# Zeros for all slot lists asked for with the first loads, and the expert weights' last row taken off on TensorE behind the first routing

## The reference, cut to what matters

```
x = in_features                                    # 8 batches x 512 rows x 128
x = x + 0.5 * moe(layernorm(x))                    # "mixture 1"
x = x + attention(layernorm(x))                    # 16 heads of 8, causal, rotary
x = x + 0.5 * moe(layernorm(x))                    # "mixture 2", same weights
x = x + 0.5 * mx_linear(layernorm(x))              # weight and input on an fp6 grid
x = x + gated_scan_block(x)                        # sigmoid/tanh scan, then a SiLU block
x = x + 0.5 * mx_linear(layernorm(x))

def moe(z):                                        # 8 experts, the best 2 for each row
    s, i = top_k(z @ router_w + router_b, 2); g = softmax(s)
    return sum over k of g[k] * (relu(z @ W1[i[k]] + b1[i[k]]) @ W2[i[k]] + b2[i[k]])
```

## Time and profile before

| | us |
|---|---|
| three runs, median (lowest to highest) | 975.32 (974.37 to 977.39) |
| the profiled execution | 978.61 |
| its span | 976.8 |
| PE busy | 837.3 (86%) |
| POOL busy | 666.3 (68%) |
| DVE busy | 623.6 (64%) |
| ACT busy | 550.1 (56%) |
| granted clock of PE, mean | 0.949 of 2.4 GHz |

### The profile page before, as it was taken

The page is one execution under the profiler, slowest core; times in us unless marked ns, Lnnn a source line. Parts: engine busy times, 40 slices in busy tenths (PEclk is TensorE's granted clock), DMA queues, the critical chain, the costliest instruction groups (busy, mean ns, idle before and its releaser), DMA issues.

```text
span 976.8 us, 23169 instructions
## 1 busy us (share of the span) xinstructions
PE 837.3 (86%) x7489; PEld 615.0 (63%) x7489; DVE 623.6 (64%) x1918; ACT 550.1 (56%) x1221; POOL 666.3 (68%) x851
## 2 busy tenths in 40 slices
PE   2279568987999999999999999999997998757884
PEld 2279568963856576564557555668975997434553
DVE  7650016267589687789978977884435346597674
ACT  2234234436576767666766767677663556744751
POOL 6728996788894337888741897884599983786342
PEclk9999869998999999999999999999998999776897
DMA  8958446583844343453444353433532771110000
GB/s 316 331 209 237 126 130 182 172 225 105 232 141 120 98 136 111 139 157 97 136 116 134 89 152 111 127 92 99 170 111 90 218 219 41 35 28 33 1 11 32
DMA packets 117271, 129.65 MB, mean 133 GB/s; under 512 B 14883, under 2 KB 84643, under 8 KB 117030
## 3 DMA queue, kind: packets, MB, share of 16 engines
q1 hardware_dynamic: 108966, 111.39, 38.8%
q0 software_dynamic: 8192, 16.79, 5.9%
HBM read 87.37 MB, written 40.37 MB: 131 GB/s over the span
## 4 chain that ended last, share of the span: by engine, by line
PE 36%; POOL 34%; DVE 12%; issue 8%; ACT 6%; DMA 3%; SPq 1%; POOLq 0%; DVEq 0%; ACTq 0%
PE bank L765 32%; POOL small L1642 10%; POOL z_scratch L1651 8%; POOL yg L1664 7%; PE bank L777 4%; POOL P L1686 4%; DVE sm_m L1277 2%; DMA yg<-y_scratch,pos 2%; POOL sm_f L1621 1%; ACT P L1441 1%; ACT P L1523 1%; DVE xs L1215 1%; POOL ab L1674 1%; DMA z_scratch<-P 1%; DVE xs L1218 1%
## 5 line engine op out<-in xcount | busy, mean ns | idle before, releaser
L1277 DVE TENSOR_REDUCE sm_m<-bank 128x4 f32<-128x512 f32 (+2 forms) x320 | 204.8, 682 | 52.3 <-PE bank L765 49.6
L1523 ACT ACTIVATE P<-bank 128x512 f32<-128x512 f32 x320 | 173.8, 596 | 32.9 <-PE bank L765 27.3
L765 PE MATMUL bank<-w2r,hb 128*128 x1360 | 188.5, 283 | 0.0
L765 PE MATMUL bank<-zt,wt 128*128 128x128 f32 x1360 | 181.5, 284 | 4.3 <-ACT zt L1466 3.4
L1686 POOL TENSOR_SCALAR_AFFINE_SELECT P<-P 128x256 f32<-128x256 f32 (+1 forms) x320 | 116.1, 383 | 96.4 <-ACT P L1523 92.6
L765 PEld LDWEIGHTS bank<-zt,wt 128*128 128x128 f32 x1360 | 166.6, 197 | 13.4 <-issue 4.8
L1651 POOL DMA_INDIRECT z_scratch<-zb,pos x128 | 131.6, 1028 | 59.5 <-issue 24.6
L765 PEld LDWEIGHTS bank<-w2r,hb 128*128 128x128 f32 x1360 | 166.2, 193 | 2.6 <-issue 0.7
L1482 ACT ACTIVATE hb<-bank 128x512 f32<-128x512 f32 x170 | 100.9, 596 | 96.2 <-PE bank L765 83.3
L1642 POOL TENSOR_TENSOR small<-small 128x4 f32<-128x4 f32 x137 | 145.4, 1061 | 10.6 <-DVE pos L1201 7.2
L1664 POOL DMA_INDIRECT yg<-y_scratch,pos x128 | 130.6, 1020 | 23.7 <-issue 20.7
(11 more groups left out here) (219 smaller groups left out, 1407.6 us busy)
## 6 DMA issues: line engine op xcount, KB each, us to landing
wt<-w_scratch SPq DMA_DIRECT2D x170, 256.0 KB
zin<-z_scratch SPq DMA_DIRECT2D x82, 128.0 KB
y_scratch<-yt SPq DMA_DIRECT2D x82, 128.0 KB
q_scratch<-qpart SPq DMA_DIRECT2D x48, 128.0 KB
k_scratch<-kpart SPq DMA_DIRECT2D x48, 128.0 KB
Ks<-k_scratch SPq DMA_DIRECT2D x64, 96.0 KB
Qs<-q_scratch SPq DMA_DIRECT2D x64, 96.0 KB
z_scratch<-P SPq DMA_DIRECT2D x6, 512.0 KB, 5.7
```

Source lines behind the costliest of these rows:

```text
L765: return e.matmul(o, lhs, rhs, start=start, stop=stop, **kw)
L1277: e.tensor_reduce(to, of, AX.X, ALU.max, negate=True).then_inc(*d_max.step(i, f"m{s_}"))
L1523: e.activation(P[:, (2 * i + s_) % PR, :], shared("scor", i, 0, s_), ACT.Exp, scale=SCALE).then_inc(*a_sc.step(i, f"e{s_}"))
```

## The change

1. SP's first loads become a stage of six steps, `begin`. Batch 1's `x` is asked for second instead of sixth, and a 128x128 matrix `less` (the identity with minus ones in its last row) is added.
2. `FIRST_FILL` and `LATER_FILL` become steps of SP's list (`zero`, `fill`) that depend on `begin` alone. `LATER_FILL` is no longer behind `zin` 5, and starts with the second list.
3. `split` moves from POOL to PE and ACT: PE multiplies W1 by `less` (128x512, fp32) and ACT copies the bank back over `P`. The loads of the last rows (eight of 256 KB) go. Its first step waits for phase 0's `route` product on PE. `last_row` goes.
4. W1 is loaded without the bias in its last row; before the first `wload`, SP copies the eight bias rows from DRAM over the rows 127 of each expert in `w_scratch`, and waits for that.
5. `route` takes both one-hot lists in one multiply and one reduction instead of two of each; `pos` and `ei` are separate steps (costs 3.3 and 1.1), and `scat` waits for the first.
6. ACT begins with an `Exp` of four numbers, ahead of anything it waits for but a memset.
7. The planner now keeps calls of `scat` in phase 0 apart by 1.35 us in its own reckoning.

```
+LATER_FILL = pieces_of(1, 0, SLOTS) + pieces_of(0, PHASE[0].blocks * SB, SLOTS)
+    "begin": ("S0.9+2.6 S0.47+2.6<-1 S1.9+2.4<-1 S1.9+2.7<-1 S0.47+2.3<-1 S0.02+0.0<-1", [], 1),
-    "sload": ("S0.95+6", [], 1),
-    "split": ("G1.25 S0.52+4", [], 1),
+    "sload": ("S0.47+4.5", [], 1),
+    "split": ("P0.97+0.2 A0.6+0.15 S0.52+4", [(0, 1)], 1),
+    "zero": ("S1.4+8", [], 1),
+    "fill": ("S2.4+10", [], 1),
-    "route": ("P0.2+0.2 D4.9+0.15",
+    "route": ("P0.2+0.2 D3.3+0.15 D1.1+0.15",
...
+        return [("sload", u, 0), ("route", 0, 0)] if k == 0 else []
+        return [("route", OF_TILE[u], 1)] + ([(("zero", "fill")[OF_TILE[u]], 0, 0)] if OF_TILE[u] < 2 else []) if k == 0 else []
...
             def sload(n):
                 e.dma_start(P[:, n, :], a["w1"][n]).then_inc(l_raw[n], 16)
-                e.dma_start(last_row(n), a["wr"][n]).then_inc(l_raw[n], 16)
-                if n == NE - 1:
-                    fill(FIRST_FILL, l_zero0)
...
-                if n == 5:
-                    fill(LATER_FILL, l_zero)
...
                 if u == 0:
                     w.wait_ge(s_w, 16 * NE)
+                    e.dma_start(wd.rearrange("(e r) c -> e r c", r=128)[:, D - 1, :], a["b1"]).then_inc(l_b1, 16)
+                    w.wait_ge(l_b1, 16)
...
+            def split(n):
+                w.wait_ge(l_less, 16)
+                w.wait_ge(l_raw[n], 16)
+                o = take("split", n, 0, a_split.at(n, "w"))
+                mm(o, less_last, P[:, n, :], True, True).then_inc(*t_split.step(n, "w"))
+                yield
...
+            def split(n):
+                w.wait_ge(*t_split.at(n, "w"))
+                e.activation(P[:, n, :], shared("split", n, 0), ACT.Copy).then_inc(*a_split.step(n, "w"))
+                yield
...
-                for k, oh in ((1, o1), (2, o2)):
-                    then(e.tensor_tensor(by_j(m_), oh[:, 0:T, :], by_j(ps), ALU.mult), f"m{k}")
-                    then(e.tensor_reduce(pf[:, k - 1, :], by_j(m_), AX.X, ALU.add), f"p{k}")
+                then(e.tensor_tensor(m_, oh[:, :, 0:T, :], by_j(ps).unsqueeze(1).to_broadcast([128, 2, T, 8]), ALU.mult), "m")
+                then(e.tensor_reduce(pf, m_, AX.X, ALU.add), "p2")
...
+            w.wait_ge(*d_init.at(0, "half"))
+            e.activation(early, mhalf, ACT.Exp)
```

More of the change, by code:

```diff
@@ L214, in follows @@
     if stage == "bias":
-        return [("first", 0, 1)] if k == 0 else []
+        return [[("first", 0, 1), ("begin", 0, 4)], [("route", 0, 1)], [], []][k]
     if stage == "res":
@@ L254, in network @@
 def network():
-    counts = {"first": 1, "xload": NB - 2, "late": 1, "sload": NE, "split": NE, "wquant": 1, "prep": 2 * NB, "route": PHASES, "scat": NTILE,
+    counts = {"begin": 1, "first": 1, "xload": NB - 2, "zero": 1, "fill": 1, "late": 1, "sload": NE, "split": NE, "wquant": 1, "prep": 2 * NB, "route": PHASES, "scat": NTILE,
               "bias": 1,
@@ L752, in mxb @@
                 yield
-            begin()
-            follow("S", {"sload": sload, "split": split, "xload": xload, "late": late, "wload": wload, "zin": zin, "res": res, "proj": proj, "stack": stack,
+            follow("S", {"begin": begin, "sload": sload, "split": split, "xload": xload, "zero": first_fill, "fill": later_fill, "late": late, "wload": wload, "zin": zin, "res": res, "proj": proj, "stack": stack,
                          "mrow": mrow, "mxb": mxb})
@@ L1047, in gated @@
                 yield
[L1049 removed]
+            follow("P", {"prep": prep, "split": split, "route": route, "zin": zin, "hid": hid, "res": res, "proj": proj,
                          "maxi": maxi, "mrow": mrow, "scor": scor, "val": val, "heads": heads, "wquant": wquant,
```

105 lines of the change are left out of this document (62 added, 43 removed), and 10 rows, old and new, of the table STAGES.

## The result

The changed kernel takes 959.29 us (957.20 to 960.55), the kernel before beside it 975.88 (974.37 to 977.39): a ratio of 0.983 (95% interval 0.980 to 0.985), 16.6 us less. I had forecast 955 (947 to 967), a gain 4 us too large. Run once more, beside other kernels, it gave 0.982 (0.980 to 0.984). The profiled execution took 957.2 us with a span of 955.4.

The account below looks back on a forecast made before the run. PE was taken to bound the middle, with time to win only at the two ends. Phase 1's first POOL call, moved from 72.05 to 51.4, should carry whole: 975.3 - 20.6 = 954.7, say 955 us, range 947 to 967.

Parts of the forecast that it names:

- The later fill costs nothing: At the start: the later zeros, asked for early, lie under phase 0's POOL work and cost nothing.
- First slots, 4.2 us: Start of POOL's phase 0: first call 4.2 us earlier, at 23.6 instead of 27.81; bounds 0.4 and 5.5.
- Phase 0 on POOL, 24.2 us: POOL's 16 calls of phase 0, with three roots instead of four, take 24.2 us instead of 25.2, ending at 47.8.
- Phase 1's slots, 51.4: POOL's first call of phase 1 comes at 51.4 instead of 72.05, set by the path from batch 4's root to `pos`.
- The weights, covered: SP's first weights asked for at 42 instead of 31.95; covered by phase 1's rows, due at 112.3, so costing nothing.
- The hole on PE, 3 to 8 us: PE's idle gap between phase 0's and phase 1's experts shrinks from 22.8 us to between 3 and 8.
- How far it carries: From phase 1's first call to the end: POOL's chain moves whole, and all 20.6 us should reach the end.
- The middle: From 250 us PE has only 20.8 us idle in 570, so work ahead that ends earlier brings the end earlier.
- carried in part: Rival, chance 0.22: newly planned lists refill the hole with one later wait of 12.6 us, giving 967 or so.
- Splitting on PE costs nothing: Early slices: splitting W1 adds about 10 us of PE work where PE is 20% busy, costing nothing.

Follow-up runs that it names:

- e1: The kernel before with only the later zeros' fill moved, to right behind the first zeros: 970.1 us, 0.991 of the kernel before.
- e2: The changed kernel with the later fill put back inside the load of the sixth pair of blocks: 974.2 us, 0.997 of the kernel before.
- e5: The changed kernel with W2 loaded right behind the bias rows and the eight other late loads behind the sixth pair's load: 956.5 us, 0.979 of the kernel before.
- e6: The changed kernel with DVE's bias-row steps moved from behind the first routing to behind the second, plan computed anew: 956.7 us, 0.979 of the kernel before.
- e7: The changed kernel with both edits, late loads taken apart and DVE's bias row behind the second routing: 951.5 us, 0.973 of the kernel before.

## Why the prediction was right or wrong

The sign and the cause were right: the zeros were the wait, and once they came early the time fell by 16.6 us of the 20.6 forecast. That the profiled execution (957.2) met the forecast for it (958.0) within a microsecond is luck: one of the two profiled executions lay above its median and the other below. By its steps:

- **The later fill costs nothing.** Right in the sum, not to the letter. In e1, where it moved alone, the end gained 8.6 us, but phase 0's experts began 4.4 us later. In the changed kernel it costs less: without it (e2) SP asks for the weights at 35.52 instead of 37.70, and phase 0's experts begin at 58.70 instead of 60.03.
- **First slots, 4.2 us.** Right but undersized: the first call moved 5.2 us, from 27.81 to 22.65 (forecast 23.6). DVE's scores began 2.5 us earlier (12.45 against 14.92), where I had 1.5.
- **Phase 0 on POOL, 24.2 us.** 48.38 - 22.65 = 25.7. Three operations took 2.01, 1.57 and 1.86 us beside DVE's bias steps, about 2.5 us more than free ones. I had allowed under 1 us for all meetings of POOL and DVE. The end of phase 0 was forecast at 47.8 and was 48.38, as the early start made up for it.
- **Phase 1's slots, 51.4.** 52.24; batch 4's root 37.47 for 36.7. Right within 0.9 us.
- **The weights, covered.** This is where it went wrong. They were asked for at 37.70, earlier than my 42. But the rows, which I had at 49.1, landed at 53.7: I took the 1.3 us of the earlier trace rows for the landing, from a stretch with the queues nearly free, and now 3.7 MB of late loads stood in them. My bound of 53.9 for the first `zin`, from SP's issuing, was met by luck: SP was done at 47.7 and then waited for the rows. The experts of phase 0 began only 0.9 us earlier. I called that covered, because their rows' successor, phase 1, was due at 112.3. It was not covered, since two other things wait for the end of these experts: batches 5 to 7 in the new lists, and the gathers, through the rows written back. e5 shows the price: 4.4 us at the start of the experts are 4.2 at the first hidden block of phase 1.
- **The hole on PE, 3 to 8 us.** PE turned `zin` at 111.86 for 112.3, a hole of 2.47 us; then came a second wait, 3.11 us, for batch 7's norm, which I had not seen.
- **How far it carries.** "POOL's chain (gathers, slots of phase 2) is moved whole, as it has no hole to absorb it" was the sentence that failed. A chain has no hole only as long as nothing else becomes later than it. Once the calls were 19.8 us earlier, the gathers met phase 0's written rows (possible near 111.8, 15.7 us earlier than the 127.49 before) and batch 7's root behind them; 12.5 us were left. Phase 1's first hidden block kept 16.5, as PE had no such need of the gathers.
- **The middle.** 20.3 us of idle time became 22.6: no place of 12.6 us was refilled, so the rival "carried in part" was not what happened. But new lists do move this number: 17.1 in e6 and e7, where the changed kernel's own lists gave 22.6 and 25.2 in two runs. So the rival's reason was sound.
- **Splitting on PE costs nothing.** Right: the 9.5 us of products lie in the first 50 us, where PE's idle time fell by 8.7, and POOL's first call was early all the same.

## What to carry to other kernels

When a wait is taken away at the head of a chain, ask for each later step what else it waits for and how early that can be; here the answer (the end of phase 0's experts at 110) was in the same trace, and capped what POOL could win. The landing of a small transfer is to be priced at the load of the queues where it now falls, not at the load where it was measured. And where a planner writes all lists anew, several us either way may come that have nothing to do with the edit (here that is argued, not shown); an edit that moves one engine's step alone does nothing if another engine's list still has it late.

## What the runs showed of the hardware

DVE steps over three partitions and 1152 elements (`scalar_tensor_tensor`, 1.40 us) held POOL's operation in flight until about 0.9 us behind their own end (0.84 to 0.92 in the changed kernel and e6), be it a small arithmetic one (1.04 becomes 2.01 to 2.19) or the issue of an indirect DMA (1.03 becomes 2.10). The Trainium skill, "SBUF — State Buffer", section "Who interferes with whom", says that two SBUF inputs on DVE keep out GpSimd operations that read SBUF; the arithmetic ones agree. It infers that one DVE operation with two SBUF inputs, `tensor_tensor`, leaves the writing of an indirect DMA's descriptors alone. It says nothing of the kind of `scalar_tensor_tensor`, and the call at 49.40, which ran beside one, took 2.10 us. Its positions (`pos`) lie in SBUF, so it may fall under the first rule instead; no run here tells the two apart.

Indirect DMAs issued by POOL 1.27 us apart, 24 in a row, brought the other engines nearly to a stop beside running experts (16 us with 3.69 us of work on PE, and a kernel 24 us slower); at 2.31 us apart, they did not, and in pairs at 1.8 us on the mean hardly (1.5 us on phase 0's experts). In phase 0 of the changed kernel they run as close, but no more than seven in a row, and no such stop was seen; little else is due there.
